# Last message-passing layer of a four-layer graph network: rows waited for in groups of four tiles, the last chunk summed by group into its own PSUM bank, the input row folded into the self product

## The reference

```python
x = _layernorm(x + _L0_gnn_ref(x, L0_gnn_weight, src, dst, edge_type_64))   # one 32x32 matrix per edge type
x = _layernorm(x + _L1_gnn_ref(x, edge_index, edge_weight))                 # sum of e * x[src]
x = _layernorm(x + _L2_gnn_ref(x, edge_index))                              # sum of x[src]
x = _layernorm(x + _L3_gnn_ref(x, edge_index, edge_attr_4, edge_attr_32, W1, b1, W2, b2, si_w0, si_w1))
```

```python
h = relu(edge_feat @ W1 + b1)                   # 32 -> 64, per edge
w = (h @ W2 + b2).reshape(e, 4, MUL, MUL)       # 256 weights per edge, MUL = 8
s_e, v_e = s[src], v[src]                       # 8 scalars, 8 vectors of 3, gathered rows
m0 = ALPHA * (einsum('ei,eio->eo', s_e * sh0, w_000) + C110 * einsum('eim,em,eio->eo', v_e, sh1, w_110))
m1 = ALPHA * (einsum('ei,em,eio->eom', s_e, sh1, w_011) + einsum('eim,eio->eom', v_e * sh0, w_101))
out = segment_sum(m0, m1 by dst) + SI_SCALE * (node row times si_w0, si_w1)
```

## Time and profile before

| | |
|---|---|
| three runs | 9516.43, 9542.63, 9567.0 us, median 9542.63 us |
| span of the profiled execution, first to last instruction | 5779.0 us |
| busy in the span | PE 4906.1, DVE 4334.3, POOL 4010.0, ACT 2952.9 us |
| last layer, from the first gather's turn to the end | about 3140 to 5779 us |
| granted TensorE clock, mean of the span | 0.735 of full speed |

### The profile page before, as it was taken

One profiled execution on the slowest core, in us unless ns is written; L12 is line 12 of the kernel. 1 busy time (PEld: TensorE's weight loads), 2 busy tenths in 40 slices (PEclk: granted clock), 3 DMA queues, 4 the chain that ended last, 5 costly groups with the idle time before them and its releaser, 6 DMA issues.

```text
span 5779.0 us, 132934 instructions
## 1 busy us (share of the span) xinstructions
PE 4906.1 (85%) x47121; PEld 3926.4 (68%) x47122; DVE 4334.3 (75%) x8266; ACT 2952.9 (51%) x7181; POOL 4010.0 (69%) x4168
## 2 busy tenths in 40 slices
PE   7788888888888886766687999999999999999997
PEld 4487887787777775443443777777777777777775
DVE  4488887888888884111111899999999999999998
ACT  5555555555555552000001666666666666666664
POOL 0677777777777777777601777777777777777774
PEclk7556655666666666777787788888888788888887
DMA  9754455656656558999996111111111111111111
GB/s 330 291 189 179 176 189 181 223 206 235 209 205 236 207 206 296 364 364 364 340 324 177 28 28 28 28 28 30 28 28 28 28 28 30 28 28 28 30 28 20
DMA packets 596624, 865.48 MB, mean 150 GB/s; under 512 B 170817, under 2 KB 418690, under 8 KB 579458
## 3 DMA queue, kind: packets, MB, share of 16 engines
q1 hardware_dynamic: 363858, 385.79, 21.3%
q10 hardware_dynamic: 99504, 406.06, 17.9%
q0 software_dynamic: 133120, 71.57, 7.3%
HBM read 455.19 MB, written 406.85 MB: 149 GB/s over the span
## 4 chain that ended last, share of the span: by engine, by line
POOL 61%; issue 21%; DMA 9%; PE 5%; DVE 2%; ACT 1%; POOLq 0%; another core or an unknown queue 0%; ACTq 0%; SPq 0%; DVEq 0%
POOL gathered L614 61%; DMA arena<-adj 5%; PE psum L1088 2%; DMA rel_table<-arena 1%; DMA arena<-counts 1%; PE psum L1058 1%; DMA table_out<-adj 1%; PE psum L952 1%; ACT table_out L666 0%; PE psum L894 0%; ACT arena L666 0%; PE psum L921 0%; DMA gathered<-rel_table,idx 0%; DMA idx<-key_i 0%
## 5 line engine op out<-in xcount | busy, mean ns | idle before, releaser
L614 POOL DMA_INDIRECT gathered<-x_rows,idx x2048 | 1943.7, 949 | 903.1 <-issue 624.6
L614 POOL DMA_INDIRECT gathered<-rel_table,idx x2048 | 2001.4, 977 | 637.9 <-issue 636.3
L1177 PE MATMUL psum<-w,arena 65*128 65x256 f32 x4096 | 1198.4, 444 | 1.9 <-DVE arena L1826 1.9
L1177 PEld LDWEIGHTS psum<-w,arena 65*128 65x128 f32 x4096 | 889.7, 225 | 274.4 <-issue 144.3
L739 ACT COPY arena<-psum 128x512 f32<-128x512 f32 x1024 | 603.0, 589 | 855.8 <-PE psum L1002 794.8
L952 PE MATMUL psum<-arena 128*128 128x184 f32 x4096 | 887.7, 376 | 8.9 <-DVE acc L1539 8.9
L952 PEld LDWEIGHTS psum<-arena 128*128 128x128 f32 x4096 | 853.4, 235 | 45.5 <-issue 9.6
L952 PE MATMUL psum<-gathered,arena 128*128 128x32 f32 x4096 | 703.5, 343 | 206.2 <-DMA gathered<-rel_table,idx 206.2
L952 PEld LDWEIGHTS psum<-gathered,arena 128*128 128x128 f32 x4096 | 692.9, 267 | 234.0 <-issue 151.1
L853 ACT ACTIVATE arena<-gathered,sh 128x32 f32<-128x32 f32 x2048 | 448.1, 307 | 528.4 <-DMA gathered<-x_rows,idx 528.4
L1826 DVE TENSOR_TENSOR arena<-psum,arena 128x256 f32<-128x256 f32 x1536 | 671.2, 492 | 0.0
(11 more groups left out here) (223 smaller groups left out, 5297.0 us busy)
## 6 DMA issues: line engine op xcount, KB each, us to landing
adj<-arena ACTq DMA_DIRECT2D x128, 2048.0 KB
arena<-adj SPq DMA_DIRECT2D x93, 2048.0 KB
counts<-arena ACTq DMA_DIRECT2D x128, 512.0 KB
arena<-counts SPq DMA_DIRECT2D x64, 1024.0 KB, 11.5
arena<-adj SPq DMA_DIRECT2D x40, 1024.0 KB
rel_table<-table_out ACTq DMA_DIRECT2D x32, 1024.0 KB, 9.9
rel_table<-arena ACTq DMA_DIRECT2D x32, 1024.0 KB, 10.0
gathered<-rel_table,idx POOLq DMA_INDIRECT x2048
```

Of the source, the lines that this page charges most:

```text
L614: pool.indirect_dma_start(gathered[:, s, j, :], None, rows[l], bass.IndirectOffsetOnAxis(ap=idx[:, s, j:j + 1], axis=0),).then_inc(rows_in ...
L1177: mm = pe.matmul(pair[g % 2][:, WN * q:WN * q + WN], hidden[:, s % 2, q, P * g:P * g + P], w2[:, :], start=True, stop=True)
```

## The change

Four edits, all for the last layer.

1. The rows of layer 3 are counted by slot and group of four tiles (`group_in[s][g]`). DVE makes `cprod` and its sum group by group inside the group loop (96 columns each), and one of the three L1826 products now stands ahead of the L1822 product. ACT scales rows group by group, for the same chunk as DVE is at and no longer for the next: group 0 ahead of `hidden_units(c+1)`, group 1 behind it, group 2 in the middle of the 16 onehot squares, group 3 behind the onehots.
2. PE runs `hidden_units(c+1)` behind group 1's edge weights, no longer behind group 0's.
3. The scatter of the last chunk goes by group, each behind its own `msg_ready`, and into `bank_t`, which then isn't used otherwise, so that it no longer waits for the sums of the chunk before.
4. `w_self` gets the identity divided by SI_SCALE added once (one small DVE instruction at the setup), so that `acc` holds the input row as well; L1375 goes, the norm reads `acc`, and its epsilon is 1e-5/ALPHA².

Semaphores of the layers are shared in other places (layers 1 and 2 use one set, the `extra` path fewer), with values moved by `BEFORE[l]`; the shared ones carry no other work here.

```diff
+        group_in = [[sem(f"group_in_{s}_{g}") for g in range(GROUP)] for s in range(SLOTS)]
...
-                    ).then_inc(rows_in[l][s], 16)
+                    ).then_inc(group_in[s][j // GROUP] if l == 3 else rows_in[l][s], 16)
...
-            def beside(c, s, it, following=True):
-
+            def chunk3(c, s, it, following=True):
+
+                scale_rows(c, s, it, 0)
                 if following:
                     hidden_units(c + 1, s + 1)
-                    scale_rows(c + 1, (s + 1) % SLOTS, it if s + 1 < SLOTS else it + 1)
-                onehots(3, c, s)
+                scale_rows(c, s, it, 1)
+                onehots(3, c, s, lambda: scale_rows(c, s, it, 2))
+                scale_rows(c, s, it, 3)
...
                     edge_weights(c, s, g)
-                    if g == 0 and following:
+                    if g == 1 and following:
                         hidden_units(c + 1)
...
-                pe.wait_ge(msg_ready, CHUNKS * GROUP + 1)
-                pe.wait_ge(added[3], CHUNKS)
-                scatter(3, SLOTS - 1, range(TILES)).then_inc(scattered[3], 1)
+                for g in range(GROUP):
+                    pe.wait_ge(msg_ready, (CHUNKS - 1) * GROUP + (g + 2))
+                    mm = scatter(3, SLOTS - 1, range(GROUP * g, GROUP * g + GROUP), bank_t)
+                mm.then_inc(scattered[3], 1)
...
+            dve.scalar_tensor_tensor(w_self[:, :], stack[:, :], 1.0 / SI_SCALE, w_self[:, :], ALU.mult, ALU.add)
...
+                whole = acc[:, 0:BLOCKS, :] if l == 3 else xn[:, :, :]
                 if l == 3:
-                    link(dve.scalar_tensor_tensor(xn[:, :, :], acc[:, 0:BLOCKS, :], ALPHA, xn[:, :, :],
-                                                  ALU.mult, ALU.add))
+                    pass
...
-                dve.wait_ge(rows_in[3][s], it * (16 * TILES) + 16 * TILES)
...
-                dve.tensor_tensor(cprod[:, :, :, :], v, sh1.unsqueeze(2).to_broadcast([P, TILES, MUL, 3]), ALU.mult
-                                  ).then_inc(cprod_ready, 1)
-                dve.wait_ge(cprod_ready, c + 1)
-                dve.tensor_reduce(zs[:, :, 0:MUL], cprod[:, :, :, :], AX.X, ALU.add).then_inc(c_ready, 1)
-                dve.wait_ge(c_ready, c + 1)
-                dve.wait_ge(z_scaled, c + 1)
...
+                    dve.wait_ge(group_in[s][g], it * (16 * GROUP) + 16 * GROUP)
+                    dve.tensor_tensor(cprod[:, tiles, :, :], v[:, tiles],
+                                      sh1[:, tiles].unsqueeze(2).to_broadcast([P, GROUP, MUL, 3]), ALU.mult
+                                      ).then_inc(cprod_ready, 1)
+
                     dve.wait_ge(w_made, c * GROUP + (g + 2 * GROUP + 1))
-
                     dve.wait_ge(q_ready, group + 1)
                     dve.tensor_tensor(prod_q[:, :, :, :], split(w[:, :, A_END:Q_END], MUL),
                                       over_o(gathered[:, s, tiles, 0:MUL], MUL), ALU.mult).then_inc(pq_ready, 1)
+                    dve.wait_ge(cprod_ready, group + 1)
+                    dve.tensor_reduce(zs[:, tiles, 0:MUL], cprod[:, tiles, :, :], AX.X, ALU.add).then_inc(c_ready, 1)
...
+                    dve.wait_ge(z_scaled, group + 1)
+                    dve.wait_ge(half_v, group + 1)
+                    product_v(0)
+                    dve.wait_ge(c_ready, group + 1)
...
-                add_chunk(3, CHUNKS - 1, SLOTS - 1, wide)
+                add_chunk(3, CHUNKS - 1, SLOTS - 1, wide, bank_t)
```

More of the change, by code:

```diff
@@ L143, in build @@
         epsc = sb("epsc", [P, 1])
+        epsc_out = sb("epsc_out", [P, 1])
         one_col = sb("one_col", [P, 1])
@@ L310, in build, with per_layer @@
         table_stored = [sem(f"table_stored_{n}") for n in range(4)]
[L311 to L317, removed]
+        rows_in = [[sem(f"rows_in_{l}_{s}") for s in range(SLOTS)] for l in ("first", "middle")]
+        rows_in.append(rows_in[1])
+        group_in = [[sem(f"group_in_{s}_{g}") for g in range(GROUP)] for s in range(SLOTS)]
+        def per_layer(name):
+            first, middle, last = [sem(f"{name}_{l}") for l in ("first", "middle", "last")]
+            return [first, middle, middle, last]
+        onehot_ready, scattered, added = [per_layer(name) for name in ("onehot_ready", "scattered", "added")]
+        windows_done = [None] + [sem(f"windows_done_{l}") for l in ("middle", "last")]
+        windows_done.insert(1, windows_done[1])
+        BEFORE = [0, 0, CHUNKS, 0]
         squared = sem("squared")
@@ L711, in normalise_part, with square_onehots, onehots @@
                                ).then_inc(part_std, 1)
-            def onehots(l, c, s):
-                act.wait_ge(windows_done[l], c + 1)
-                for j in range(TILES):
+            def square_onehots(l, c, s, tiles):
+                for j in tiles:
                     a = act.activation(onehot[:, s % 2, j, :], iota1[:, :], ACT.Square, scale=-1.0,
                                        bias=key_all[:, bass.ds(c * TILES + j, 1)])
-                a.then_inc(squared, 1)
+                return a
+            def onehots(l, c, s, beside=None):
+                act.wait_ge(windows_done[l], BEFORE[l] + c + 1)
+                square_onehots(l, c, s, range(TILES // 2))
+                if beside is not None:
+                    beside()
+                square_onehots(l, c, s, range(TILES // 2, TILES)).then_inc(squared, 1)
                 act.wait_ge(squared, act.snap(squares))
@@ L946, in _, with scatter @@
             pe.wait_ge(setup, SETUP_BASE)
-            def scatter(l, s, tiles):
+            def scatter(l, s, tiles, bank=bank_s):
                 for j in tiles:
                     message = msg[:, s % 2, j, :] if l == 3 else gathered[:, s, j, :]
-                    mm = pe.matmul(bank_s[:, 0:message.shape[-1]], onehot_of(l, s)[:, j, :], message,
+                    mm = pe.matmul(bank[:, 0:message.shape[-1]], onehot_of(l, s)[:, j, :], message,
                                    start=(j == 0), stop=(j == TILES - 1))
@@ L1238, in _ @@
             dve.memset(epsc[:, :], 1e-5)
+            dve.memset(epsc_out[:, :], 1e-5 / (ALPHA * ALPHA))
             dve.memset(one_col[:, :], 1.0)
@@ L1823, in messages @@
                                       over_o(zs[:, tiles, 0:2 * MUL], 2 * MUL), ALU.mult).then_inc(a_ready, 1)
-                    dve.wait_ge(half_v, group + 1)
-                    for m in range(3):
-                        last = dve.tensor_tensor(
-                            prod_v[:, :, m], split(w[:, :, Q_END:WN], MUL),
-                            over_o(zs[:, tiles, ZC + m:5 * MUL:3], MUL), ALU.mult)
-                    last.then_inc(pair_free, 1)
+                    product_v(1)
+                    product_v(2).then_inc(pair_free, 1)
                     to = msg[:, s % 2, tiles]
```

78 lines of the change are left out of this document (41 added, 37 removed).

## The result

| | before | changed |
|---|---|---|
| median, 13 runs each | 9542.63 us (9502.2 to 9580.1) | 9491.69 us (9463.38 to 9520.02) |
| ratio | | 0.9944, 95% interval 0.9928 to 0.996 |
| span of a profiled execution | 5779.0 us | 9495.5 us |
| granted TensorE clock, mean | 0.735 | 0.607 |

The account below looks back on a forecast made before the run. POOL's gathers were taken to bound the last layer, DVE trailing. Catching up 27.0, scatter 6.8 and L1375 2.3 sum to 36.1 us: 9542.6 - 36.1 = 9506.5 us; own range 9498 to 9514, full range 9464 to 9560.

Parts of the forecast that it names:

- The 3763.6 us between span and runs I take as unchanged: Whole kernel: run time outside the profiled span stays, so 36.1 us comes off 9542.6, giving 9506.5.
- The rival that the saving is hidden by time outside the span: Whole kernel: the saving is hidden anyway by time outside the span; chance 0.03.
- POOL-bound, DVE a fixed distance behind: Last layer: POOL's gathers set 20.06 to 20.08 us a chunk; DVE's last message ends 31.8 us after the last row.
- no cost, with 0.6 us to spare: PE in each chunk: hidden_units behind group 1 delays group 2's weights, 11.7 us against DVE's 12.3.
- The catching up, -27.0 us: Layer's end: DVE, waiting by group, gets locked to the gathers; messages end at 5718.5, 27.0 us earlier.
- rival (a): Last layer: no catching up, the new ACT and PE order holds DVE at 19.9 to 20.1 us a chunk; 9528, chance 0.15.
- The split instructions, +0.1 to +0.3 us a chunk: DVE in each chunk: four 96-column pairs replace L1804 and L1807, mostly overlapped, costing +0.1 to +0.3 us.
- (b): DVE in each chunk: small instructions don't overlap, +0.86 us, period 20.20, DVE becomes the bound; 9550, chance 0.08.
- (c): DVE's sequencer: four more waits per chunk before short instructions make it slower, period 21.1 us; chance 0.05.
- same instructions; no gain, no loss.: POOL and SP: only the gathers' semaphore differs, so the pace stays 20.06 to 20.08 us a chunk.
- The late item, group 1's scaled rows behind the hidden units: ACT in each chunk: ready 7.2 us after group 0's rows, DVE wants them at 5.1; costs only DVE's slack.
- The scatter by group and the fold, -6.8 and -2.3: Kernel's end: last scatter and sums shrink from 10.1 to 3.3 us (6.8 us); removing L1375 saves 2.3 us.

Follow-up runs that it names:

- e1: Kernel before, unchanged, profiled again: ran 5789.29 us, span 5787.4 us.
- e8: Kernel before, unchanged, profiled once more on another chip: ran 9569.11 us, span 9567.3 us.
- e10: Kernel before with 4 of a chunk's 16 tiles left out of the last layer's loop scatter: 9265.91 us against 9516.53, ratio 0.9745.
- e12: Kernel before plus hidden_units behind group 1, last scatter by group into bank_t, input row folded into w_self; rows awaited by chunk: 5772.21 us, ratio 0.9983.
- e4: Kernel before plus only the last scatter by group into bank_t and the input row folded into w_self: 5773.06 us against 5780.78, ratio 0.9986.
- e9: Kernel before with only PE's hidden_units moved behind group 1's edge weights: 9437.38 us against 9516.53, ratio 0.9912.
- e2: Changed kernel with PE's hidden_units back behind group 0: 5758.11 us, ratio 0.996 to the kernel before (5780.78).
- e11: Changed kernel with PE's hidden_units back behind group 0, run again in another set: 5757.13 us, ratio 0.9959 to the kernel before (5781.84).
- e5: The changed kernel itself, run on another chip: 9532.89 us, ratio 0.9943 to the kernel before (9582.99).
- e6: Kernel before plus only rows by group with the new DVE/ACT order and hidden_units behind group 1: 9508.76 us against 9582.99, ratio 0.9916.

## Why the prediction was right, and where not

*"The 3763.6 us between span and runs I take as unchanged"* is the step that failed. e1 and e8 show that these microseconds aren't outside the span: they are the same kernel under another condition, in which the gathers no longer run back to back, PE and DVE start late in a part of every chunk, and less work on PE makes the layer shorter (e10). The profile gave a sign that was left aside: a span of 5779.0 against runs of 9516 to 9567 (front table) had no source in the rows, and rows from inside that span needn't describe the runs; in e1 and e8 span and run differ by under 2 us. The number 9507 came from adding the gain of one condition to the time of another. With -36 foretold and -51 measured, by another edit than the one that was to bring most of it, it stands inside its range by luck: 9491.7 is below the own range of 9498 to 9514, and only the spread added on both sides takes it in. The rival that the saving is hidden by time outside the span fell with it: there is no such time.

*POOL-bound, DVE a fixed distance behind*: right at 5780 us (e1: POOL idle for issue alone, as in the earlier trace rows); wrong for the runs that were forecast, where POOL waits 1172.7 us in 3000 for indices.

*PE's `hidden_units`: "no cost, with 0.6 us to spare".* This edit was priced at nothing, because POOL covered it. At 5780 that holds (e12 and e4). At 9540 the cover is gone and the edit is the gain, 0.93 us a chunk in e9's profile, 119 over 128 chunks (against e8, another chip of that kind), 79 us in the medians on one chip (0.9877 to 0.9947, 50 to 117 us). The prediction had the wait that it relieves in view, 0.7 us of DVE a chunk, and gave no price for the case that PE's time counts.

*The catching up, -27.0 us.* At 5780: the mechanism is right, by e2 and e11. The distance from the last gather to the last addition fell by 28 to 32 us; the forecast's part of it is 27.0 + 6.8 = 33.8. The last message alone ends 12.0 us (e2) and 8.7 us (e11) behind the start of the last gather, before it was 34.2 and 33.7: 22 to 26 us of the 27.0. In the runs forecast it did not take place: 71.4 us from last gather to `acc` in the changed kernel, 74.9 in e8. That is what rival (a) says of the distance, with another cause than it gives.

*The split instructions, +0.1 to +0.3 us a chunk, (b) and (c) against it.* Right at both conditions. In the changed kernel:

```profile
7200.43 0.25 DVE L1831 TENSOR_TENSOR cprod<-gathered,sh 128x96 f32<-128x96 f32 x1
7200.60 0.42 DVE L1837 TENSOR_TENSOR arena<-psum,gathered 128x256 f32<-128x256 f32 x1
```

0.17 us from start to start with a length of 0.25, as in the earlier trace rows, and a semaphore wait between them. DVE's bare period in e2 is 19.2 us, 19.8 where a loop round ends, as before the split; the +0.1 to +0.3 don't show. The Trainium skill's rule that the next instruction waits until the pipe is empty ("VectorE: DVE Perf Modes", section on the DRAIN) is not what these rows show. The same section adds, which the prediction left out, that a next instruction which isn't held starts earlier; these rows agree with that, 0.17 us behind the start of one of 0.25.

*POOL: "same instructions; no gain, no loss."* Wrong by 18 us at 5780, more than half of the catching up, in the two profiles. The instruction was the same, its neighbour on DVE was not. The prediction counted waits and lengths of each engine by itself; the 558/590 spread of L1804 beside a gather was the only hint.

*The late item, group 1's scaled rows behind the hidden units.* Right in place. In the changed kernel:

```profile
7212.73 0.94 ACT L870 ACTIVATE arena<-gathered,sh 128x32 f32<-128x32 f32 x4
7213.71 0.50 DVE L1844 TENSOR_TENSOR arena<-psum,arena 128x256 f32<-128x256 f32 x1 [2.26 <-ACT arena L870]
```

It costs DVE 148.4 us in 66 waits here, and isn't in the kernel before. It may be why e9, without it, came out ahead of e5, but that wasn't tested alone.

*The scatter by group and the fold, -6.8 and -2.3.* 9.5 us in e4's profile, 7.7 in its medians. The fold alone is not shown by its medians.

*What the sum becomes at 5780.* From the profiles: catching up and scatter -28 to -32, the fold -1.9, slower gathers +17 to +21 (2586.7 and 2588.2 against 2567.4 and 2569.5), pair by pair together -12 to -14. e2's and e11's medians say -22.7 and -24.7, with intervals that reach from -32 to -16. The profiles are one execution each, and the layer's start alone differs by 7.5 us between two of the kernel before (3143.9 and 3151.4), and the profiled runs of e2 and e11 were 12.7 and 10.9 us above their medians. So these are not in conflict; in which stage the typical run is shorter than the profiled one is not known.

**Open.** Why the two conditions differ, whether it is the chip or the moment, and whether the late starts are instructions that come late or semaphores that arrive late: the slow stretch follows the gathers in phase in e5, e8, e9 and e10, but no run changed the gathers and kept the rest. The changed kernel itself was not run at 5780 us; e2 and e11 differ from it by edit 2. Edit 1's own worth at 9540 us is within the intervals (e6, e9).

**The best version.** At 9540 us that is e9, one line moved, 0.9912 against the changed kernel's 0.9944 and 0.9943, with overlapping intervals; e6 with 0.9916 can't be told from it. At 5780 us it is e2 with 0.996. Which is better depends on the condition.

## What to carry to other kernels

When the span of the profile and the time of the runs differ by more than some microseconds, the profile is of another condition: get one whose span agrees with the time to be changed before a sum is made from it. An edit costed at nothing because another engine covers it should be given a price for the case that the cover goes; here that edit was the whole result. When DVE work is divided, look at what its pieces run beside, too.

## What the runs showed of the hardware

- The same kernel takes 5780 us on one chip and 9517 to 9583 on others, with its DVE and ACT instructions as long as before (L1804 558 ns on both; the activations of L853 307 and 310 ns). Of the 3780 us between e1 and e8, 3669 lie in the stretches with gathers. The difference lies in late starts and in PE: the granted clock, a mean over its two levels of 1.2 and 2.4 GHz, was 0.82 of full speed in the last layer of e1, where PE was 93% busy, and 0.65 in e8, where it was 73% busy with gaps of up to 2 to 3 us. DVE's L1819 started, in e8, 12.7 us a chunk later than its weights were ready, and 0.3 us in e1.
- In the 9540 us condition ACT's wait for its own instruction's end took 1.83 us on average and up to 7.4 (e8), in the 5780 us condition 0.12 us (e1). PE's unexplained gaps in e8 end 12 to 24 us behind each chunk's first gather.
- In the kernel before, a gather that started while the 558 ns instruction L1804 was running took 1087 ns on average, up to 1319; one within which L1804 started took 944.
